# A ninth count table in a graph network's edge aggregation: 117 gather steps in place of 121

## The chip, the core and the metric

The kernel runs on one core of one Trainium2 chip. The metric is the device time of one execution in microseconds, as the median of several runs; before the change it is 1335.8 us. The core's engines are TensorE (PE, with its weight loads as PEld), VectorE (DVE), ScalarE (ACT), GpSimd (POOL) and SyncE (SP). Each works through a queue of its own in order, and they meet at semaphores.

## The reference, cut to what matters

One layer of a graph network with linear attention and a mixture of experts, on 6250 nodes of 256 features and 100,000 edges that are sorted by their target node. The change lies in the graph part:

```
src_f, dst_f = concat(src, loop), concat(dst, loop)
h   = layernorm(x) @ W
deg = segment_sum(1, dst_f);  dinv = rsqrt(deg)
out = segment_sum(h[src_f] * dinv[src_f] * dinv[dst_f], dst_f) + conv_bias
...
x = x + graph(out) + attention(layernorm(x))
x = x + experts(layernorm(x))
```

The target nodes are drawn as 6250 times the square of a uniform number. So the first edges, in sorted order, share few targets, and further on a run of edges spreads over more and more of them.

## The kernel before, in words

Phases follow each other with a barrier between them: loads, degrees and the normed rows z (written to `table` in memory); then the edge phase, lines 719 to 1277, in which the attention and a residual sum are computed beside the edges; then the feature product, the router and the experts. `acc` holds the sums per target node, features on partitions.

The 196 edge groups of 512 edges (four chunks of 128) are summed in two ways.

- **Gathers.** A group is a *step* q of the edge phase: GpSimd gathers the 512 source rows with four indirect DMAs (line 811) into 16 slots, four steps deep, so it waits (`pe_done`) only when it is four steps ahead. VectorE builds four one-hot masks of the targets (`onehots`, line 1045). TensorE multiplies rows and masks, 16 matmul records a step in two halves (`aggregate`, line 828), into a window of 96 nodes. VectorE adds the window to `acc` (`add`, line 1058).
- **Count tables.** For the first groups, where the targets lie close, the edges are counted instead. A table covers one entry of `DBLK` and at most 128 target nodes: `adj`, 128 targets by 6250 sources. For each chunk VectorE builds two one-hots (lines 1073, 1074), TensorE multiplies them (`count`, line 839), and VectorE adds the counts at the chunk's offset (`chunk_add`, line 1088). `DWB` is how many targets a chunk may span. A finished table is multiplied by all of z: 49 products (`product`, line 851), each with 128 rows of z that the sync queue loads in 128 KB pieces into six buffers (`z_rows`, line 775). The result is copied by ScalarE (line 1002), turned by TensorE (line 858) and added to `acc` by VectorE (line 1066). Two buffers `adj` take turns; ScalarE wipes one behind its products (line 958).

Before, eight tables cover groups 0 to 74, and `GQ` = 121 groups go through gathers.

The order is written by hand over the steps. Each engine walks through q = 0 to GQ - 1 and in each through four quarters, and `share(q, lo, hi, n)` deals n items evenly over the steps lo to hi:

- chunks of table b over `BUILT[b]` to `BUILT[b+1]`, its products over `USED[b]` to `USED[b+1]`;
- keys of 49 tiles over steps 0 to 11 (`A0, A1`; line 865 on TensorE, 1099 on VectorE), then setup products at steps 12 and 13;
- keys and values with their context over steps 14 to 33 (`C0, C1`; lines 874 and 881), then a chain of small setup steps at 34 to 36;
- queries of 49 tiles over `B0` to `B1` (lines 888, 896, 902 on TensorE, 1120 to 1145 on VectorE);
- the residual sum over `D0` to `D1`, with one load of x per tile behind the z loads on the sync queue (line 781).

Within a quarter TensorE does counts, attention, products and then, in every second quarter, half of the aggregation. Ahead of the last step the sync queue issues four late loads, after the last table but one has been turned.

Of the kernel before, what the change touches and what calls it, by code (L numbers as in the profile page):

```python
# [7 lines left out]
P = 128  # L8
# [6 lines left out]
T = -(-N // P)  # L15
# [11 lines left out]
OHR = 4  # L27
ECOL = E // P
assert OHB % OHR == 0 and ECOL < NC and E - ECOL * P <= P
DBLK = ((0, 27), (27, 38), (38, 46), (46, 53), (53, 59), (59, 65), (65, 70), (70, 75))  # L30
ND = DBLK[-1][1]
NDB = len(DBLK)
DWB = (5, 5, 6, 7, 8, 8, 8, 9)
DW = max(DWB)
DLIM = P - DW
MD = ND * GC
RUNS = [(min(g0 for (g0, _), k in zip(DBLK, DWB) if k == d), max(g1 for (_, g1), k in zip(DBLK, DWB) if k == d), d)
        for d in sorted(set(DWB))]
assert all((d - 1) * -(-WIN // d) < WIN for d in DWB) and list(DWB) == sorted(DWB) and T * DW <= 512
GQ = NG - ND  # L40
# [27 lines left out]
def build(nc, a_x, a_src, a_dst, a_gw, a_cb, a_lnw, a_lnb, a_pre, a_wqkv, a_mk, a_mv, a_wout, a_bout,  # L68
# [6 lines left out]
    with ExitStack() as ctx:  # L75
        def sb(name, shape, dt=f32):
            return ctx.enter_context(nc.sbuf_tensor(name, shape, dt))
# [11 lines left out]
        R1 = sb("R1", [P, T * D])  # L89
# [4 lines left out]
        zT = R2[:, :].rearrange("p (k n) -> p k n", k=KC)  # L94
        y_all = x_all
        o_all = x_all
        adj = [R1[:, b * T * P:(b + 1) * T * P].rearrange("p (j n) -> p j n", n=P) for b in range(2)]

        def o_tile(t):

# [66 lines left out]
        small = sb("small", [P, 64])  # L167
# [41 lines left out]
        root3, val3, tmp3 = (RG[:, 3660 + 3 * T * k:3660 + 3 * T * (k + 1)] for k in range(3))  # L209
        negmean, total_x = sd[:, :], sa[:, :]  # L210
        iwin_i = slotb[:, 1, 0:P].bitcast(i32)
        cols = sb("cols", [P, 16])
        least, cut, bad = (sb(name, [P, GC]) for name in ("least", "cut", "bad"))
        inblk = S_t[:, :, :, :].rearrange("p s c w -> p (s c w)")[:, 500:500 + P]
        isd = sb("isd", [P, 2])
# [28 lines left out]
        with nc.Block(no_gpsimd_drain=True) as block:  # L244
# [164 lines left out]
            def _(pool):  # L409
                n = 0  # L410

                def step(ins):
                    nonlocal n
                    n += 1
                    ins.then_inc(pl, 1)
                    pool.wait_ge(pl, n)
# [11 lines left out]
                step(nc.gpsimd.memset(inblk, 0.0))  # L428
                for a, b in DBLK:
                    step(nc.gpsimd.tensor_copy(inblk[:, a:b], ident[:, a:a + 1].to_broadcast([P, b - a])))  # L430
# [251 lines left out]

        A0, A1 = 0, 12
        C0, C1 = 14, 34
        B0, B1 = 37, 88
        D0, D1 = 91, GQ - 2
        BUILT = (0, 33, 47, 61, 74, 86, 95, 104, 112)
        USED = (33, 47, 61, 74, 86, 95, 104, 112, GQ - 2)

        def share(q, lo, hi, n):  # L690

            if not lo <= q < hi:
                return range(0)
            return range(n * (q - lo) // (hi - lo), n * (q - lo + 1) // (hi - lo))
# [6 lines left out]
        def chunks(q):  # L701

            for (g0, g1), lo, hi in zip(DBLK, BUILT, BUILT[1:]):
                for m in share(q, lo, hi, (g1 - g0) * GC):
                    yield g0 * GC + m

        def products(q):

            for b in range(NDB):
                for j in share(q, USED[b], USED[b + 1], T):  # L710
                    yield b, j
# [4 lines left out]
        def block_of(m):  # L716
            return next(b for b, (g0, g1) in enumerate(DBLK) if m < g1 * GC)

        phase = later
        with nc.Block(no_gpsimd_drain=True) as block:  # L720
# [96 lines left out]
            def _(pe):  # L817
# [15 lines left out]
                def count(m):  # L833

                    pe.wait_ge(key_ok, m + 1)
                    if m >= 2:
                        pe.wait_ge(cnt_ok, m - 1)
                    wide = T * DWB[block_of(m)]
                    nc.tensor.matmul(psK[m % 2][:, 0:wide], hots[m % 4], hotk[m % 4][:, 0:wide], start=True,  # L839
# [14 lines left out]
                def turn_block(b):  # L854

                    pe.wait_ge(blk_cp, b + 1)
                    for k in range(KC):
                        last = nc.tensor.transpose(psD[:, D + k * P:D + (k + 1) * P], block_rows(b)[:, k, :], ident[:, :])
                    last.then_inc(blk_t, 1)
# [83 lines left out]
                for q in range(GQ):  # L943
                    if q in USED[1:]:
                        turn_block(USED.index(q) - 1)
                    for r in range(4):
# [9 lines left out]
            def _(act):  # L956
# [47 lines left out]
                for q in range(GQ):  # L1004
                    if q in USED[1:] and USED.index(q) - 1 < NDB - 2:
                        b = USED.index(q) - 1
                        act.wait_ge(blk_t, b + 1)
# [30 lines left out]
            def _(v):  # L1038
# [21 lines left out]
                def add_block(b, groups):  # L1060

                    at = nc.vector.value_load(first_i[0:1, DBLK[b][0]:DBLK[b][0] + 1], min_val=0, max_val=N - 1)
                    v.wait_ge(blk_t, b + 1)
                    v.wait_ge(acc_ok, groups)
                    win = acc[:, :, bass.ds(at, P)]
                    nc.vector.tensor_tensor(win, win, halved(psD[:, D:2 * D]), ALU.add).then_inc(blk_ok, 1)

                def chunk_onehots(m):

                    if m >= 4:  # L1070
                        v.wait_ge(cnt_ps, m - 3)
                    wide = T * DWB[block_of(m)]
                    nc.vector.tensor_scalar(hotk[m % 4][:, 0:wide], iokey[:, 0:wide], key[:, m:m + 1], None, ALU.is_equal)
# [187 lines left out]
                for q in range(GQ):  # L1261
                    if q in USED[1:]:
                        add_block(blocks, q - 1)
# [889 lines left out]
```

## Time and profile before

| | |
|---|---|
| median of 3 runs | 1335.8 us (1331.95 to 1337.17) |
| profiled execution | 1330.7 us, span 1329.0 us |
| PE / PEld busy | 1205.2 / 1075.8 us |
| DVE / ACT / POOL busy | 911.8 / 544.3 / 785.8 us |
| gathers in the edge phase (POOL, line 811) | 476, from 126.1 to 738.7 us |
| edge phase | from about 126 to 763 us |
| experts (bound by PE) | from about 926 us to the end |

The chain that ended last is TensorE in the experts, back to 926 us. It does not reach back into the edge phase, which the barrier at 763 us ends, so the edge phase is read from its own rows: by the times of single steps, and by who waits there for whom. The granted clock of TensorE is full from 139 us to the last tables, apart from short stretches.

### The profile page before, as it was taken

To read this page: it belongs to the slowest core of one execution; us is meant where nothing else is said; L and a number is where in the kernel's file an instruction comes from. 1 tells how busy PE (TensorE), PEld (TensorE's weight loads), DVE (VectorE), ACT (ScalarE), POOL (GpSimd) and SP (SyncE) were. 2 spreads that over 40 slices of the span, in tenths; PEclk is the share of its full clock that TensorE was granted. 3 is DMA by queue.
4 is the path that set the end of the run, shared out by engine and by line. 5 is a ranking of instruction groups with operands and counts; after the bars stand their busy time and mean duration, and the time that the engine had idled before them with its cause. 6 is when DMAs were issued, how large, how long until landed. Compare 5 with 4: busy or idle time off the path is not lost. (4 is left out here: it accounts for less than half of the span.)

```text
span 1329.0 us, 29794 instructions
## 1 busy us (share of the span) xinstructions
PE 1205.2 (91%) x8333; PEld 1075.8 (81%) x8334; DVE 911.8 (69%) x2764; ACT 544.3 (41%) x1402; POOL 785.8 (59%) x757
## 2 busy tenths in 40 slices
PE   6974989998999999999898698956999999999998
PEld 6964978887889889887786546944999999999997
DVE  8997987887888777788783268888444444444444
ACT  8737102221333333333311102545555555555553
POOL 7105777777777777777776200002476666666665
PEclk9997999999999999999998899965999999999999
DMA  8026333336666667789898601577254444444443
GB/s 254 0 85 192 100 104 104 104 109 198 195 199 203 200 201 206 209 255 280 268 292 261 218 0 34 173 241 238 53 79 68 70 69 69 70 69 71 71 68 43
DMA packets 138889, 190.11 MB, mean 143 GB/s; under 512 B 22261, under 2 KB 116956, under 8 KB 138532
## 3 DMA queue, kind: packets, MB, share of 16 engines
q0 software_dynamic: 43440, 90.29, 29.4%
q1 hardware_dynamic: 95348, 98.64, 23.4%
q8 instruction: 43, 0.70, 0.2%
q14 instruction: 58, 0.48, 0.1%
HBM read 156.37 MB, written 33.44 MB: 143 GB/s over the span
## 5 line engine op out<-in xcount | busy, mean ns | idle before, releaser
L811 POOL DMA_INDIRECT RG<-table,srci x476 | 465.2, 977 | 149.7 <-issue 139.6
L828 PEld LDWEIGHTS ps<-S_t,RG 128*128 128x128 f32 x1936 | 254.6, 195 | 20.6 <-DMA RG<-table,srci 10.4
L828 PE MATMUL ps<-S_t,RG 128*128 128x96 f32 x1936 | 257.6, 276 | 8.0 <-DMA RG<-table,srci 7.4
L851 PE MATMUL ps<-zrow,R 128*128 128x256 f32 (+1 forms) x784 | 219.9, 388 | 20.1 <-DMA zrow<-table 13.3
L2100 POOL DMA_INDIRECT out<-R,S_t x105 | 166.1, 1582 | 99.3 <-DVE R L2070 55.8
L1983 PE MATMUL ps<-R,RG 128*128 128x128 f32 x1680 | 206.7, 277 | 0.0
L1993 PE MATMUL ps<-R 128*128 x840 | 198.5, 379 | 0.0
L1983 PEld LDWEIGHTS ps<-R,RG 128*128 128x128 f32 x1680 | 197.7, 193 | 0.3 <-issue 0.3
L2016 ACT ACTIVATE R<-ps,RG 128x128 f32<-128x128 f32 x420 | 119.7, 367 | 175.5 <-PE ps L1983 175.5
L1088 DVE TENSOR_TENSOR R<-R,ps 128x245 f32 (+4 forms) x300 | 142.0, 473 | 70.6 <-PE ps L839 45.4
L2066 DVE TENSOR_TENSOR R<-ps,R 128x256 f32<-128x256 f32 x105 | 44.6, 425 | 202.0 <-PE ps L1993 202.0
L851 PEld LDWEIGHTS ps<-zrow,R 128*128 128x128 f32 (+1 forms) x784 | 137.1, 192 | 45.5 <-DMA zrow<-table 23.2
L1993 PEld LDWEIGHTS ps<-R 128*128 128x128 f32 x840 | 151.7, 190 | 16.3
L958 ACT ACTIVATE R<-iwin 128x256 f32<-128x256 f32 (+2 forms) x152 | 71.5, 476 | 186.3 <-PE ps L851 174.7
L2088 POOL DMA_INDIRECT R<-ntable,S_t x105 | 103.9, 990 | 40.2 <-issue 29.3
L2025 ACT ACTIVATE RG<-R 128x1028 f32 x105 | 112.7, 1075 | 9.7 <-PEq L86 9.7
L1678 POOL COPY R<-R 128x8 f32<-128x8 f32 (+1 forms) x13 | 6.0, 474 | 145.8 <-DVEq L1846 126.5
L2055 DVE TENSOR_SCALAR R<-ps,gamma,beta 128x128 f32<-128x128 f32 x212 | 76.2, 400 | 0.0
L487 PE MATMUL ps<-R 128*128 128x49 bf16 x784 | 73.8, 269 | 0.0
L487 PEld LDWEIGHTS ps<-R 128*128 128x128 bf16 x784 | 70.9, 145 | 2.7 <-DVE R L562 2.6
L1045 DVE TENSOR_TENSOR S_t<-dstrel,iwin 128x384 f32<-128x384 f32 x121 | 66.9, 553 | 0.8
L1074 DVE TENSOR_SCALAR ohs<-iokey,slo 128x128 bf16<-128x128 f16 x225 | 61.9, 275 | 0.0
(371 smaller groups left out, 1817.3 us busy)
## 6 DMA issues: line engine op xcount, KB each, us to landing
zrow<-table SPq DMA_DIRECT2D x384, 128.0 KB
RG<-table,srci POOLq DMA_INDIRECT x484, 3.4
ntable<-R SPq DMA_DIRECT2D x12, 516.0 KB, 7.0
out<-R SPq DMA_DIRECT2D x12, 512.0 KB, 3.2
table<-R SPq DMA_DIRECT2D x9, 640.0 KB
R<-in_x SPq DMA_DIRECT2D x6, 896.0 KB, 10.0
R<-in_w SPq DMA_DIRECT2D x8, 514.0 KB, 6.5
slot<-in_x SPq DMA_DIRECT2D x32, 128.0 KB, 4.1
```

What stands on the lines that cost most here:

```text
L487: last = nc.tensor.matmul(ps[7][:, 0:T], ohlo[k][:, :, c], ohhi[k][:, :, c], start=False, stop=False)
L811: nc.gpsimd.indirect_dma_start(out=grows[:, s, :], out_offset=None, in_=table, in_offset=bass.IndirectOffsetOnAxis(ap=srci[:, ND + q, c:c ...
L828: last = nc.tensor.matmul(window(q % 2)[:, h, :], grows[:, s, h * P:(h + 1) * P], S_t[:, q % 2, c, :], start=c == 0, stop=c == GC - 1)
L851: nc.tensor.matmul(psD[:, 0:D], adj[b % 2][0:n, j, :], zrow[0:n, i % ZR, :], start=j == 0, stop=j == T - 1).then_inc(z_used, 1)
L1088: nc.vector.tensor_tensor(win, win, psK[m % 2][:, 0:T * wide].rearrange("p (j w) -> p j w", w=wide), ALU.add).then_inc(cnt_ok, 1)
L1983: last = nc.tensor.matmul(psH[s % 2][:, h * P:(h + 1) * P], w1r[:, s, k * HID + h * P:k * HID + (h + 1) * P], ur[:, s % 2, k, :], start=k ...
L1993: last = nc.tensor.matmul(psY[s % 2][:, 0:D], hr[:, s % 2, h, :], w2_sb[:, bass.ds(e, 1), h, :].rearrange("p a f -> p (a f)"), start=h == ...
L2016: last = act.activation(hr[:, s % 2, h, :], psH[s % 2][:, h * P:(h + 1) * P], ACT.Gelu, bias=w1r[:, s, KC * HID + h:KC * HID + h + 1])
L2025: act.activation(w1r[:, s, :], w1_sb[:, bass.ds(e, 1), :].rearrange("p a f -> p (a f)"), ACT.Copy).then_inc(c_ok, 1)
L2055: nc.vector.tensor_scalar(ur[:, s % 2, k, :], psX[s % 2][:, k * P:(k + 1) * P], gamma[:, k:k + 1], beta[:, k:k + 1], ALU.mult, ALU.add)
L2088: nc.gpsimd.indirect_dma_start(out=xr[:, t % 4, :], out_offset=None, in_=ntable, in_offset=bass.IndirectOffsetOnAxis(ap=gat[:, t:t + 1], a ...
L2100: nc.gpsimd.indirect_dma_start(out=a_out, out_offset=bass.IndirectOffsetOnAxis(ap=sct[:, t:t + 1], axis=0), in_=yr[:, t % 4, :], in_offset ...
```

## The change

The four groups 75 to 78 move from gathers to a ninth table: `ND` goes from 75 to 79, `GQ` from 121 to 117, gathers from 484 to 468, chunks from 300 to 316, products from 392 to 441. With four steps fewer, all that is dealt over steps is dealt anew: the first table is built in 29 steps and not 33, the tables' products run in 12, 12, 11, 10, 10, 9, 8, 7 and 7 steps, where they ran in 14, 14, 13, 12, 9, 9, 8 and 7, and the queries and the residual sum have two steps less each. With an odd number of tables the two `adj` buffers swap places, so that the last table again lies in the upper half of R1, and `cols` moves into `small`. Keys, and keys and values, keep their steps.

```
-DBLK = (..., (65, 70), (70, 75))
+DBLK = (..., (65, 70), (70, 75), (75, 79))
-DWB = (5, 5, 6, 7, 8, 8, 8, 9)
+DWB = (5, 5, 6, 7, 8, 8, 8, 9, 9)
...
-        adj = [R1[:, b * T * P:(b + 1) * T * P].rearrange("p (j n) -> p j n", n=P) for b in range(2)]
+        adj = [R1[:, (b + NDB) % 2 * T * P:((b + NDB) % 2 + 1) * T * P].rearrange("p (j n) -> p j n", n=P) for b in range(2)]
...
-        cols = sb("cols", [P, 16])
+        cols = small[:, 8:17]
...
-        B0, B1 = 37, 88
-        D0, D1 = 91, GQ - 2
-        BUILT = (0, 33, 47, ..., 104, 112)
+        B0, B1 = 37, 86
+        D0, D1 = 89, GQ - 2
+        BUILT = (0, 29, 41, ..., 101, 108)
...
```

What this does to TensorE's order shows at two places. The first is step 31, its first half, in the stretch of the keys and values (L874, context L881), with counts (L839) and the half aggregation (L828) at its end. Before:

```order
L839 MATMUL ps<-ohk,ohs 128x245
L874 MATMUL ps<-wqkv,R 128x256 x2
L881 MATMUL ps<-vsl,esl 128x129
L839 MATMUL ps<-slot,ohs 128x245
L874 MATMUL ps<-wqkv,R 128x256 x2
L881 MATMUL ps<-vsl,esl 128x129
L828 MATMUL ps<-S_t,RG 128x96 x4
```

The same half step on TensorE in the changed kernel:

```order
L839 MATMUL ps<-slot 128x245
L874 MATMUL ps<-wqkv,R 128x256 x2
L881 MATMUL ps<-vsl,esl 128x129
L851 MATMUL ps<-zrow,R 128x256
L839 MATMUL ps<-ohk,ohs 128x245
L874 MATMUL ps<-wqkv,R 128x256 x2
L881 MATMUL ps<-vsl,esl 128x129
L851 MATMUL ps<-zrow,R 128x256
L828 MATMUL ps<-S_t,RG 128x96 x4
```

Two products (L851) of the first table stand between what was there; before, they began at step 33.

The second place is step 70 on TensorE, in the stretch of the queries (L888, with L896 and L902), from its first count to its second half of the aggregation. Before:

```order
L839 MATMUL ps<-slot 128x343
L851 MATMUL ps<-zrow,R 128x256
L888 MATMUL ps<-wqkv,R 128x128 x2
L896 MATMUL ps<-ident,ksl 128x128
L902 MATMUL ps<-wout,vsl 128x256
L851 MATMUL ps<-zrow,R 128x256
L828 MATMUL ps<-S_t,RG 128x96 x4
L839 MATMUL ps<-ohk,ohs 128x343
L851 MATMUL ps<-zrow,R 128x256 x2
L828 MATMUL ps<-S_t,RG 128x96 x4
```

The same step on TensorE in the changed kernel:

```order
L839 MATMUL ps<-slot,ohs 128x392
L851 MATMUL ps<-zrow,R 128x256
L888 MATMUL ps<-wqkv,R 128x128 x2
L896 MATMUL ps<-ident,ksl 128x128
L902 MATMUL ps<-wout,vsl 128x256
L851 MATMUL ps<-zrow,R 128x256 x2
L828 MATMUL ps<-S_t,RG 128x96 x4
L839 MATMUL ps<-slot 128x392
L851 MATMUL ps<-zrow,R 128x256 x2
L828 MATMUL ps<-S_t,RG 128x96 x4
```

The step has five products where it had four, and its chunks belong to a later and wider table (392 columns for 343).

## Rows read from the trace of the kernel before

**Rows 1.** The gathers, line 811: durations in ns, first and last start; idle time's releasers.

```profile
L811 POOL DMA_INDIRECT RG<-table,srci x476: 940/946/1543, 126.1 to 738.7; - x159
...
  issue: 139.6, 458
  PE ps L828: 8.7, 17
```

**Rows 2.** Busy time of each engine in stretches of the edge phase, then clock and DMA.

```profile
core 0: us, PE busy (x) PEld busy (x) DVE busy (x) ACT busy (x) POOL busy (x), PEclk, DMA share, GB/s
139.00:203.00 64.00, 58.53 (x456) 52.21 (x454) 57.92 (x215) 1.43 (x5) 48.77 (x51) 0.97 0.35 103
...
139.00:565.00 426.00, 401.30 (x2810) 362.57 (x2808) 347.56 (x1273) 116.03 (x393) 324.10 (x335) 1.00 0.56 165
372.00:437.00 65.00, 63.78 (x454) 59.31 (x453) 54.47 (x209) 23.99 (x82) 49.46 (x52) 1.00 0.68 203
```

**Rows 3.** Timeline of DVE, adds (steps 0, 12, 28, 33, 36, 40, 47, 59, 85): start, duration.

```profile
139.10 0.35 DVE L1058 TENSOR_TENSOR R<-R,ps 128x192 f32 x1
...
194.97 0.35 DVE L1058 TENSOR_TENSOR R<-R,ps 128x192 f32 x1
...
276.83 0.36 DVE L1058 TENSOR_TENSOR R<-R,ps 128x192 f32 x1 [0.16 <-issue]
...
303.21 0.35 DVE L1058 TENSOR_TENSOR R<-R,ps 128x192 f32 x1
...
318.83 0.36 DVE L1058 TENSOR_TENSOR R<-R,ps 128x192 f32 x1 [0.53 <-issue]
...
340.13 0.35 DVE L1058 TENSOR_TENSOR R<-R,ps 128x192 f32 x1 [0.34 <-issue]
...
376.03 0.36 DVE L1058 TENSOR_TENSOR R<-R,ps 128x192 f32 x1 [0.36 <-issue]
...
431.80 0.35 DVE L1058 TENSOR_TENSOR R<-R,ps 128x192 f32 x1 [0.36 <-issue]
...
565.16 0.36 DVE L1058 TENSOR_TENSOR R<-R,ps 128x192 f32 x1 [0.37 <-issue]
```

**Rows 4.** Timeline of PE, step 50: count, product, queries, product, half an aggregation.

```profile
386.79 0.29 PE L839 MATMUL ps<-ohk,ohs 128*128 128x294 bf16 x1
386.92 0.59 PE L851 MATMUL ps<-zrow,R 128*128 128x256 f32 x2
387.35 0.61 PE L888 MATMUL ps<-wqkv,R 128*128 128x128 f32 x4
...
388.34 0.59 PE L851 MATMUL ps<-zrow,R 128*128 128x256 f32 x2
388.77 1.03 PE L828 MATMUL ps<-S_t,RG 128*128 128x96 f32 x8
389.63 0.29 PE L839 MATMUL ps<-slot,ohs 128*128 128x294 bf16 x1
```

**Rows 5.** Timeline of PE, step 25: from keys and values to what follows their context.

```profile
257.28 1.03 PE L874 MATMUL ps<-wqkv,R 128*128 128x256 f32 x4
...
258.38 1.03 PE L828 MATMUL ps<-S_t,RG 128*128 128x96 f32 x8
```

**Rows 6.** Timeline of DVE, step 12: two chunk adds, the one-hots between them left out.

```profile
187.12 0.41 DVE L1088 TENSOR_TENSOR R<-R,ps 128x245 f32 x1
...
188.01 0.41 DVE L1088 TENSOR_TENSOR R<-R,ps 128x245 f32 x1
```

**Rows 7.** Timeline: adds of steps 94, 103 and 111; turn of the last table.

```profile
611.48 0.34 DVE L1058 TENSOR_TENSOR R<-R,ps 128x192 f32 x1
...
659.55 0.35 DVE L1058 TENSOR_TENSOR R<-R,ps 128x192 f32 x1
...
703.65 0.35 DVE L1058 TENSOR_TENSOR R<-R,ps 128x192 f32 x1
...
752.10 0.69 PE L858 MATMUL ps<-ident,R 128*128 128x128 f32 x2 [2.90 <-ACT R L1002]
```

**Rows 8.** The page's line of the products: busy, mean ns of one, idle before, releasers.

```profile
L851 PE MATMUL ps<-zrow,R 128*128 128x256 f32 (+1 forms) x784 | 219.9, 388 | 20.1 <-DMA zrow<-table 13.3 <-DVE R L1066 5.5 <-DVEq L1200 1.1
```

More of the change, by code:

```diff
@@ L29 @@
 assert OHB % OHR == 0 and ECOL < NC and E - ECOL * P <= P
-DBLK = ((0, 27), (27, 38), (38, 46), (46, 53), (53, 59), (59, 65), (65, 70), (70, 75))
+DBLK = ((0, 27), (27, 38), (38, 46), (46, 53), (53, 59), (59, 65), (65, 70), (70, 75), (75, 79))
 ND = DBLK[-1][1]
 NDB = len(DBLK)
-DWB = (5, 5, 6, 7, 8, 8, 8, 9)
+DWB = (5, 5, 6, 7, 8, 8, 8, 9, 9)
 DW = max(DWB)
@@ L684, in build @@
         C0, C1 = 14, 34
-        B0, B1 = 37, 88
-        D0, D1 = 91, GQ - 2
-        BUILT = (0, 33, 47, 61, 74, 86, 95, 104, 112)
-        USED = (33, 47, 61, 74, 86, 95, 104, 112, GQ - 2)
+        B0, B1 = 37, 86
+        D0, D1 = 89, GQ - 2
+        BUILT = (0, 29, 41, 53, 64, 74, 84, 93, 101, 108)
+        USED = (29, 41, 53, 64, 74, 84, 93, 101, 108, GQ - 2)
         def share(q, lo, hi, n):
```

## The prediction

> **What bounds the kernel now.** I read the page's slices first, then the stretch from 126 to 763 us in which GpSimd gathers, then who waits for whom there. That stretch is the only one that the change alters, and the one after it starts when it is over, so what it gains or loses is gained or lost in the time.
>
> GpSimd issues 476 of its 484 gathers here, and they run without a pause: 458 of its gaps are its own, 139.6 us over all (0.3 us each), and it waited 8.7 us for TensorE [rows 1]. From 126.1 to 738.7 us are 119 steps, 5.15 us each. So GpSimd looks like the bound, and four steps fewer look like 20.6 us. The second look is at TensorE: between 139 and 565 us it is busy for 401.3 of 426 us and VectorE for 347.6 [rows 2]. A matmul's busy time says little of the room left, so I timed the steps by the row with which VectorE adds a step's window to the sums [rows 3]: the adds of steps 0, 12, 28, 33, 36, 40, 47, 59 and 85. Steps 48 to 59 took 55.8 us, 4.65 each, below GpSimd's 5.15: there TensorE caught up on rows that had been gathered long before. Before them it had lost ground: steps 37 to 40 took 5.3 each, 29 to 33 5.3. It has hardly more room than GpSimd.
>
> **Prices.** On TensorE, start to start in a stretch without idle time [rows 4]: a chunk count 0.13 us, a product 0.43, the queries of one tile with the two matmuls behind them 0.99 (387.35 to 388.34), half of a step's aggregation 0.86, so 1.72 a step. Keys and values of one tile with their context take 1.10 (257.28 to 258.38) [rows 5]. On VectorE one chunk (an add and two one-hots) takes 0.89 (187.12 to 188.01) [rows 6]. Check: steps 48 to 59 hold 1.72 + 1.02 x 0.99 + 3.5 x 0.43 + 2.29 x 0.13 = 4.54 us by these prices and took 4.65, so 0.11 a step is not in them.
>
> **The change part by part, against the profiled run.** Removed: four steps, 16 gathers and 4 x 1.72 = 6.9 us of aggregation. Added: 49 products, 21.1 us, 16 counts, 2.1 us, and on VectorE 16 chunks, 14.2 us, less four steps' adds and one-hots. TensorE thus does some 16 us more in four steps less. Where it falls decides.
>
> Steps 1 to 12. The first table's 108 chunks lie in 29 steps instead of 33, 3.72 a step for 3.27. VectorE sets the pace there (busy for 57.9 of 64 us from 139 to 203 [rows 2]), so 12 x 0.45 x 0.89 = +4.8.
>
> Steps 13 to 28, keys and values. Here TensorE waits for ScalarE and VectorE in turn. The same 0.45 chunk costs at least TensorE's 0.13 and at most VectorE's 0.89: 0.06 to 0.40 a step. I take 0.2, since both engines have some room: +3.2 (0.9 to 6.4).
>
> Steps 29 to 33. The first table's products now start at step 29 in place of 33, and the keys and values still run to step 33. A step holds 1.72 + 2.45 x 1.10 + 4.08 x 0.43 + 3.67 x 0.13 = 6.65 us. Five are 33.3; they took 26.4 [rows 3]: +6.9. The gathered rows that wait in four steps' slots would cover this once, if TensorE came there with a lead. It comes 8 us late.
>
> Steps 34 to 36 (a chain of small setup steps between TensorE and VectorE): 0.58 product and 0.53 chunk more each, +1.0. Steps 37 to 40, bound by VectorE with 3.67 chunks for 3.14: 0.53 x 0.89 = 0.47, four times, +2.0. So the add of step 40 comes 17.9 us later, at 358.0.
>
> Steps 41 to 83. The queries run in 49 steps in place of 51, 1.05 us a step. Steps 41 to 52, 53 to 63 and 64 to 83 hold 4.08, 4.45 and 4.9 products each (the second, the third, and the fourth and fifth table), with 2.67, 2.55 and 2.4 chunks: 4.88 us (12 steps), 5.02 (11) and 5.19 (20), each with the 0.11 of the check: 59.9 + 56.4 + 106.0 = 222.3. At a change of table TensorE waited 0.8 us for VectorE (5.5 us in 7 times [rows 8]), four times 3.2. Sum 225.5: the add of step 83 at 583.5. The same point of the work before, with four tables' products left, is the add of step 85 at 565.2: **+18.3 us**, although two steps fewer lie ahead of it. GpSimd alone would have it 10.3 us earlier, so gathers now wait for TensorE.
>
> Steps 84 to the end. Before, these four tables took 46.3, 48.0, 44.1 and 48.5 us [rows 7] in 9, 9, 8 and 7 steps; now 9, 8, 7 and 7. The first was paced by GpSimd. Now rows lie ready, and TensorE needs 9 x (1.72 + 2.34 + 0.29 + 0.23 + 0.11) + 0.8 = 43.0. The others were paced by the rows of z, which come through six buffers and for which TensorE waited 13.3 us on the page [rows 8]. With 8 steps I take the 44.1 of before; with 7 steps and chunks still to build 46 (36 if the rows were there in time, 48.5 as the last table before); the last 48.5. Sum 181.6 for 186.9: **-5.3**. One z load more per row of the table goes to the sync queue ahead of the x tiles; that is in these times.
>
> At no cost: the wipes of one more table (ScalarE waits for products most of the time), the buffers that swap places, the columns moved into another tile, one more mask in the setup, and the four late loads, which keep their place behind the last table but one. If a wipe were late, VectorE's first add of a table would wait, and TensorE with it.
>
> **Sum: +18.3 - 5.3 = +13.0.** The profiled run took 1330.7 us (span 1329.0), 0.4% under the median of 1335.8. I add the difference to the median: **1349 us**. Its own range is 1339 to 1362: steps 13 to 28 at their bounds (-2.3, +3.2), steps 41 to 83 without any wait (-7.9) or with as much as steps 13 to 28 have (5.12 us for 4.84 by the prices, +7), the 7-step table (-10, +2.5). The ends of single terms don't come together, so I cut it there.
>
> **Rivals.** A. GpSimd stays the bound, and the kernel is faster. The waits of TensorE ahead of step 84 are filled by the new products, and the point of step 84 comes 10.3 us earlier by GpSimd's pace, with 5.3 behind it: 1320; all four steps in full give 1315. It holds if the waits that TensorE now has in steps 1 to 36 all but vanish. For it: TensorE's weight loads are busy for 362.6 of 426 us, 85%, against 59.3 of 65 us, 91%, where it ran without a pause [rows 2]: room for 28 us, of which 10 go with the two steps, and the work added by step 83 is 49 x 0.43 + 24 x 0.13 - 2 x 1.72 = 20.8. Against it: that room lies where TensorE waits for a chain, in steps 1 to 36, and new products start at step 29. Chance 0.18.
>
> The Trainium skill, Perfetto Trace Analysis, section Identifying the Most-Contended Engine, says to judge TensorE's headroom by the share of LDWEIGHTS time, not of matmul time. By that rule alone the added work nearly fits and A would come out, at 1320 in place of 1349. The trace agrees that matmul time says little (94% and 98% busy in those two stretches [rows 2]); whether the room can be filled, no row shows.
>
> B. The excess ahead of step 40 is only the 4.8 of VectorE: in steps 13 to 40 products run in the gaps that the chains leave, and 13 us of the sum go. 1336, no difference to be measured. For it: TensorE and VectorE alternate in waiting there, so work for one can lie in the other's time. Against it: 6.65 us of pure work in a step that has 5.15. Chance 0.22.
>
> C. The z rows bind all three last tables: two of 7 steps at 48.5 and the one of 8 at 48, and the first at its old 46.3: +10, 1359. Chance 0.10, on the forecast's side.
>
> That the change does not do what it says is excluded by the program: 468 gathers stand in it, and a chunk's 128 edges near edge 40,000 span some 7 nodes by the reference's distribution, under the nine columns.
>
> **Chances.** Forecast 0.50, C 0.10, B 0.22, A 0.18. About 0.5% is what a measurement tells from no change: faster 0.18, same 0.22, slower 0.60. The range of 1320 to 1364 leaves out the better half of A and the far end of C.
>
> **What would show it.** In the new profile: adds of step 12 near 200 us, of step 33 near 318, of step 40 near 358, of step 83 near 583; GpSimd's waits for TensorE far above 8.7 us; TensorE's waits for gathered rows gone before step 84. If the add of step 83 stands at 555 or less, the prices of steps 29 to 83 are wrong and A holds; an add of step 40 near 345 is B's. If the last four tables take 190 us or more, C is right.

## The result, and the profile after

The changed kernel takes 1353.7 us in the median of 4 runs (1353.4 to 1357.1), beside 1336.0 us before in the same series (1332.0 to 1337.2): a ratio of 1.014, 95% interval 1.012 to 1.016. It is 17.7 us slower; 13 were predicted. The profiled execution has a span of 1351.9 us.

The page's lines of the gathers, the aggregation and the products in the changed kernel, with busy time, mean ns, and the idle time before them with what ended it; of before, [rows 1] has the gathers and [rows 8] the products, and the aggregation's line stands below:

```profile
L811 POOL DMA_INDIRECT RG<-table,srci x460 | 446.2, 970 | 189.3 <-issue 124.7
L828 PE MATMUL ps<-S_t,RG 128*128 128x96 f32 x1872 | 246.6, 276 | 0.2 <-DVE S_t L1045 0.2
L851 PE MATMUL ps<-zrow,R 128*128 128x256 f32 x882 | 245.8, 389 | 25.2 <-DMA zrow<-table 16.9
```

```profile
L828 PE MATMUL ps<-S_t,RG 128*128 128x96 f32 x1936 | 257.6, 276 | 8.0 <-DMA RG<-table,srci 7.4
```

What GpSimd waited for from 126 to 790 us (total us, times, longest):

```profile
POOL RG L811 <- PE ps L828: 63.2, 50, 3.9
```

GpSimd waited 63.2 us for TensorE, where it had waited 8.7, and the aggregation (L828), which waited 7.4 us for gathered rows, waits for none. The products waited 16.9 us for rows of z (13.3 before).

The adds of steps 0, 12, 28, 33, 36, 40, 83, 92, 100 and 107 on VectorE, which answer to [rows 3] and [rows 7] (start, duration), and TensorE's turn of the last table:

```profile
142.34 0.35 DVE L1058 TENSOR_TENSOR R<-R,ps 128x192 f32 x1
...
204.48 0.36 DVE L1058 TENSOR_TENSOR R<-R,ps 128x192 f32 x1
...
290.56 0.36 DVE L1058 TENSOR_TENSOR R<-R,ps 128x192 f32 x1 [0.41 <-issue]
...
322.17 0.35 DVE L1058 TENSOR_TENSOR R<-R,ps 128x192 f32 x1
...
342.00 0.35 DVE L1058 TENSOR_TENSOR R<-R,ps 128x192 f32 x1 [0.52 <-issue]
...
365.00 0.36 DVE L1058 TENSOR_TENSOR R<-R,ps 128x192 f32 x1 [0.36 <-issue]
...
589.36 0.36 DVE L1058 TENSOR_TENSOR R<-R,ps 128x192 f32 x1 [0.37 <-issue]
...
636.78 0.34 DVE L1058 TENSOR_TENSOR R<-R,ps 128x192 f32 x1
...
682.75 0.34 DVE L1058 TENSOR_TENSOR R<-R,ps 128x192 f32 x1
...
727.70 0.35 DVE L1058 TENSOR_TENSOR R<-R,ps 128x192 f32 x1
...
775.23 0.69 PE L858 MATMUL ps<-ident,R 128*128 128x128 f32 x2 [2.92 <-ACT R L1002]
```

Differences of these rows and of those of before give the stretches (us):

| steps | before | predicted | after |
|---|---|---|---|
| 1 to 12 | 55.9 | 60.7 | 62.1 |
| 13 to 28 | 81.9 | 85.1 | 86.1 |
| 29 to 33 | 26.4 | 33.3 | 31.6 |
| 34 to 36 | 15.6 | 16.6 | 19.8 |
| 37 to 40 | 21.3 | 23.3 | 23.0 |
| 41 to 83 (before: to 85) | 225.0 | 225.5 | 224.4 |
| from there to the last turn | 186.9 | 181.6 | 185.9 |
| **first add to last turn** | **613.0** | **626.1** | **632.9** |

So 19.9 us were lost from the first add on: 21.0 up to step 83, and 1.1 came back. Another 3.2 us of the difference between the two profiles is a later first add (142.34 for 139.10), which is not the change's (last section).

Busy times (PE, PEld, DVE, ACT, POOL, with counts), granted clock, DMA share and GB/s of the changed kernel in steps 29 to 33, 34 to 36, 41 to 83 and in the last four tables. A granted clock of 1.00 is the higher of its two levels, 2.4 GHz, and 0.50 the lower, 1.2 GHz; 0.91 is a mean of both:

```profile
290.56:322.17 31.61, 31.61 (x212) 28.61 (x211) 21.21 (x75) 10.13 (x33) 18.25 (x20) 1.00 0.56 164
322.17:342.00 19.83, 15.25 (x95) 12.79 (x94) 13.62 (x51) 2.90 (x7) 12.31 (x14) 0.91 0.57 169
365.00:589.36 224.36, 222.17 (x1509) 203.61 (x1509) 190.22 (x682) 84.04 (x286) 165.61 (x172) 1.00 0.73 216
589.36:775.20 185.84, 161.61 (x945) 136.08 (x944) 117.91 (x330) 49.50 (x113) 116.32 (x118) 0.97 0.87 266
```

TensorE is busy for all of steps 29 to 33 and for 99% of steps 41 to 83. In the last tables it idles for 24 us.

### The profile page after: what moved, and what is told of

It reads as the page before. It is cut to its first block and busy times, and to the rows that moved or that the text cites. A ratio compares the mean times of both kernels' runs of the same rounds, so it can differ in the third digit from the quotient of the medians.

```text
span 1351.9 us, 30078 instructions
## 1 busy us (share of the span) xinstructions
PE 1222.7 (90%) x8385; PEld 1086.9 (80%) x8386; DVE 926.2 (69%) x2805; ACT 551.7 (41%) x1428; POOL 775.8 (57%) x742
## 5 line engine op out<-in xcount | busy, mean ns | idle before, releaser
L811 POOL DMA_INDIRECT RG<-table,srci x460 | 446.2, 970 | 189.3 <-issue 124.7
L851 PE MATMUL ps<-zrow,R 128*128 128x256 f32 x882 | 245.8, 389 | 25.2 <-DMA zrow<-table 16.9
L828 PEld LDWEIGHTS ps<-S_t,RG 128*128 128x128 f32 x1872 | 247.1, 196 | 10.0 <-DVE S_t L1045 0.6
L828 PE MATMUL ps<-S_t,RG 128*128 128x96 f32 x1872 | 246.6, 276 | 0.2 <-DVE S_t L1045 0.2
L1088 DVE TENSOR_TENSOR R<-R,ps 128x245 f32 (+4 forms) x316 | 151.4, 479 | 73.3 <-PE ps L839 48.1
L851 PEld LDWEIGHTS ps<-zrow,R 128*128 128x128 f32 x882 | 154.5, 192 | 56.6 <-DMA zrow<-table 29.8
L958 ACT ACTIVATE R<-iwin 128x256 f32<-128x256 f32 (+2 forms) x177 | 81.6, 467 | 207.7 <-PE ps L851 191.7
L839 PE MATMUL ps<-ohk,ohs 128*128 128x245 bf16 (+4 forms) x158 | 47.5, 302 | 26.0 <-DVE ohs L1074 21.5
L1074 DVE TENSOR_SCALAR ohs<-iokey,slo 128x128 bf16<-128x128 f16 x237 | 66.8, 282 | 0.0
```

The source lines that it names most:

```text
L811: nc.gpsimd.indirect_dma_start(out=grows[:, s, :], out_offset=None, in_=table, in_offset=bass.IndirectOffsetOnAxis(ap=srci[:, ND + q, c:c ...
L828: last = nc.tensor.matmul(window(q % 2)[:, h, :], grows[:, s, h * P:(h + 1) * P], S_t[:, q % 2, c, :], start=c == 0, stop=c == GC - 1)
L851: nc.tensor.matmul(psD[:, 0:D], adj[b % 2][0:n, j, :], zrow[0:n, i % ZR, :], start=j == 0, stop=j == T - 1).then_inc(z_used, 1)
L958: return act.activation(adj[b % 2][:, j:j + n, :], iwin[:, :].unsqueeze(1).to_broadcast([P, n, P]), ACT.Copy, scale=0.0)
L1088: nc.vector.tensor_tensor(win, win, psK[m % 2][:, 0:T * wide].rearrange("p (j w) -> p j w", w=wide), ALU.add).then_inc(cnt_ok, 1)
```

## The experiments

The theory: up to step 83 TensorE, with VectorE, sets the pace and GpSimd no longer does; what is lost by step 40 stays lost; the last four tables wait for rows of z. Steps are timed from the add of step 0, so that the different starts fall out.

**1. No gathers behind the fourth step, in the changed kernel.**

```
-                for q in range(EARLY, GQ):
+                for q in range(EARLY, 4):
...
-                            pe.wait_ge(got[s], (q // 4) * 16 + 16)
+                            pe.wait_ge(got[s], 16)
```

> The changed kernel, with gathers issued for the first four steps only; every later step multiplies the rows of those steps again, so the gathered rows of later steps are left out of the computation. TensorE's and VectorE's work is unchanged, GpSimd and its transfers are idle. Theory (TensorE, with VectorE, sets the pace up to step 83): the add of step 83 stays 447 us behind that of step 0, 3 us either way, and the last four tables, which wait for rows of z, gain at most 15 us from the transfers that are gone. Rival (the gathers still set the pace somewhere before step 83, through GpSimd or through the transfers that they share with the rows of z): the add of step 83 comes 10 us or more earlier.

Measured: 1330.7 us. The adds of steps 0 and 83:

```profile
139.65 0.34 DVE L1058 TENSOR_TENSOR R<-R,ps 128x192 f32 x1
...
585.63 0.36 DVE L1058 TENSOR_TENSOR R<-R,ps 128x192 f32 x1 [0.36 <-issue]
```

The add of step 83 stands 446.0 us behind the first (447.0 with the gathers): no gather sets the pace there. From step 83 to the last turn it took 166.0 us in place of 185.9, a gain of 19.8 where at most 15 were expected: without the gathers' traffic the wait for rows of z falls from 16.9 to 5.7 us.

**2. The same edit in the kernel before.**

> The kernel before with the same edit: gathers for the first four steps only, the rows of later steps left out of the computation. Theory: here the gathers did set the pace in places, so the add of step 85, 426 us behind that of step 0, comes 8 to 18 us earlier: the waits for rows go, TensorE's work stays. The first of the last four tables, 46.3 us, falls to about 43. Rival (the gathers were no bound before either, and the change lost only by added TensorE work): the add of step 85 moves less than 3 us.

Measured: 1306.6 us. The adds of steps 0 and 85:

```profile
142.68 0.35 DVE L1058 TENSOR_TENSOR R<-R,ps 128x192 f32 x1
...
559.62 0.36 DVE L1058 TENSOR_TENSOR R<-R,ps 128x192 f32 x1 [0.37 <-issue]
```

The add of step 85 stands 416.9 us behind the first, 9.1 earlier than with gathers (426.1). All but 1.1 of it arises behind step 60: before, the rows gathered ahead were used up there, and GpSimd set the pace. The first of the last four tables took 44.9 us (46.3), not the 43 expected.

Put side by side, the two runs split the loss up to step 83. Without gathers the changed kernel needs 445.98 - 416.94 = 29.04 us more: that is what the added work costs on TensorE and VectorE, with the waits of one for the other. The gathers add 1.05 us to it, where they added 9.12 to the kernel before. 29.04 + 1.05 - 9.12 = 20.97. The change did free GpSimd, but that was worth 8 us, and it paid 29.

**3. Rows of z loaded once, in the changed kernel.**

```
                     if i >= ZR:
                         sp.wait_ge(z_used, i - ZR + 1)
+                    if i >= ZR:
+                        return
...
-                    pe.wait_ge(z_in[i % ZR], i // ZR * 16 + 16)
+                    pe.wait_ge(z_in[i % ZR], 16)
```

> The changed kernel, with the rows of z loaded into the six buffers once and never again; later products multiply whatever lies there, so 435 of 441 loads of z and the right products are left out of the computation. Theory: up to step 83 nothing waits for z rows and the time is the same, 447 us from the first add to that of step 83, 5 us either way; the last four tables, which measured 186 us, fall to 155 to 165, since then TensorE's work, some 4.7 us a step at 5 to 7 products, is all that is left. Rival (traffic of the z loads slows gathers and so TensorE throughout): the add of step 83 comes 10 us or more earlier. Rival (the last tables are bound by TensorE's work as well): they stay above 178 us.

Measured: 1331.2 us. Step 83 at 446.5 us (447.0): the transfers of z slow nothing before it. From there to the last turn 155.5 us in place of 185.9. So 30 us of the last tables come with the loads of z. Here the last gathers became late instead, as what TensorE waited for most from 589 to 760 us shows (total us, times, longest):

```profile
PE ps L830 <- DMA RG<-table,srci: 7.1, 4, 3.0
```

**4. The first table's products cut to 8 columns, in the changed kernel.**

```
+                    w = 8 if b == 0 and 0 < j < T - 1 else D
-                    nc.tensor.matmul(psD[:, 0:D], adj[b % 2][0:n, j, :], zrow[0:n, i % ZR, :], ...
+                    nc.tensor.matmul(psD[:, 0:w], adj[b % 2][0:n, j, :], zrow[0:n, i % ZR, 0:w], ...
```

> The changed kernel, with 47 of the 49 products of the first table cut from 256 columns to 8; their waits, weight loads and rows of z stay, the rest of those products is left out of the computation. These are the products that now begin at step 29, among the keys and values. Two records of a product start 0.43 us apart at 256 columns; at 8 columns the weight load is what is left, by the records of 96 columns at most 0.22. So TensorE's work in steps 29 to 40 falls by 10 us or a little more. Theory (TensorE's columns are what made steps 29 to 40 late): the add of step 41 comes 8 to 12 us earlier, and most of that is still there at step 83. Rival (VectorE's chunks or the weight loads set the pace there): at most 3 us at step 41. Rival (it is made up later, the queries being bound by something else): 8 to 12 us at step 41, under 3 us at step 83.

Measured: 1357.4 us. Step 33 came 3.7 us earlier, step 41 only 1.2. None of the three cases can be read from it, because the clock moved. Busy times in steps 29 to 33, 34 to 36 and 37 to 40; the granted clock is the number before the last two:

```profile
291.31:319.10 27.79, 27.24 (x215) 25.70 (x215) 20.76 (x74) 9.86 (x33) 18.69 (x20) 1.00 0.63 188
319.10:339.15 20.05, 16.37 (x84) 15.43 (x84) 13.71 (x51) 2.90 (x7) 11.81 (x14) 0.60 0.56 164
339.15:364.42 25.27, 21.81 (x141) 20.93 (x140) 18.88 (x74) 5.71 (x17) 17.22 (x18) 0.78 0.60 180
```

With the clock at 0.60 and 0.78 the lighter steps 34 to 40 took longer than the full ones (45.3 us for 42.8). The experiment is void; the next one asks the question the other way round.

**5. The first table's products done twice, in the changed kernel.**

```
+                    if b == 0 and 0 < j < T - 1:
+                        nc.tensor.matmul(psD[:, 0:D], adj[0][0:n, j, :], zrow[0:n, i % ZR, :], start=False, stop=False)
```

> The changed kernel, with 47 of the 49 products of the first table done twice, so that this table is added to the sums twice over: that is the part that changes in the computation. TensorE has 47 x 0.43 = 20.2 us more to do in steps 29 to 40 and is never less busy than before, so that its clock has no reason to fall; nothing else is added. Theory (TensorE sets the pace of steps 29 to 33 and, with the set-up chain and VectorE, of steps 34 to 40): steps 29 to 33 grow by 5 x 4.08 x 0.43 = 8.8 us, one for one, steps 34 to 40, where TensorE now idles for some 8 us, by 4 to 11, and all of it, 13 to 20 us, is still there at step 83. Rival (VectorE sets the pace from step 29 to 40): under 6 us at step 40. Rival (there is room behind step 40 in which it is caught up): under 6 us at step 83.

Measured: 1363.2 us. Busy times in steps 29 to 33, 34 to 36, 37 to 40 and 41 to 83:

```profile
290.64:330.53 39.89, 39.89 (x248) 35.81 (x246) 21.41 (x74) 9.95 (x33) 18.37 (x20) 1.00 0.44 128
330.53:350.34 19.81, 18.66 (x121) 16.25 (x120) 13.74 (x52) 2.97 (x8) 12.18 (x14) 1.00 0.63 169
350.34:376.32 25.98, 25.40 (x168) 22.80 (x167) 19.20 (x73) 5.47 (x18) 16.07 (x17) 1.00 0.61 173
376.32:600.74 224.42, 222.23 (x1509) 203.67 (x1509) 190.21 (x683) 84.10 (x286) 165.93 (x173) 1.00 0.72 216
```

Steps 29 to 33 grew by 8.3 us, with 20 more products in that stretch, 8.6 us at 0.43 each: TensorE sets their pace, nearly one for one. Steps 34 to 36 did not move (19.8) with 12 more products, 5.2 us, in them: TensorE's waits there fell from 4.4 to 1.1 us, and its clock was 1.00 in place of 0.91. Steps 37 to 40 grew by 3.0. The sum at step 40 is 11.3 us, under the 13 to 20 expected, since I had not seen how much of steps 34 to 36 is waiting; at step 83 it is 11.4. What is lost by step 40 is carried, to a tenth, past 43 more steps. Behind step 83 4 us of it came back, where the last tables wait for transfers anyway.

**6. VectorE's chunk adds of the first two tables cut to 5 columns, in the changed kernel.**

```
-                    win = adj[b % 2][:, :, bass.ds(at, wide)]
+                    tiles = 1 if b < 2 else T
+                    win = adj[b % 2][:, 0:tiles, bass.ds(at, wide)]
```

> The changed kernel, with VectorE's chunk adds of the first two tables cut from 245 columns to 5; the counts for the other 240 columns are left out of the computation, the one-hots and TensorE's counts stay. One add took 0.41 us, and what is left may take 0.1 to 0.15, so VectorE has 1.0 us less to do in each of the steps 1 to 40. Theory (VectorE's chunks set the pace of steps 1 to 12, share in steps 13 to 28, and hold TensorE up in steps 34 to 40; in steps 29 to 33 TensorE is busy without a gap): the add of step 12, 62.1 us behind that of step 0, comes 5 to 9 us earlier, steps 13 to 28 (86.1) gain 2 to 6, steps 29 to 33 (31.6) under 1, steps 34 to 40 (42.9) 2 to 6, and from there the lead stays, 8 to 20 us at step 83. Rival (TensorE sets the pace in steps 13 to 40 as well, or the chain of keys, values and setup does): the gain is under 10 us at step 40 and comes from steps 1 to 12 alone.

Measured: 1348.5 us. Steps 1 to 12 gained 2.5 us (59.7), steps 13 to 28 2.8, steps 29 to 33 0.1, steps 34 to 40 1.5; 6.9 at step 40, 5.2 at step 83. VectorE has a part in the early steps, but a smaller one than I expected: its busy time in steps 1 to 12 fell from 55.3 to 44.9 us and the time by 2.5. Behind VectorE stands TensorE, which in these steps waits for several small things in turn (counts, keys, setup). The rival (under 10 us at step 40) has the size right, not the place.

**7. The early chunk pace alone, in the kernel before.**

```
-        BUILT = (0, 33, 47, 61, 74, 86, 95, 104, 112)
+        BUILT = (0, 29, 47, 61, 74, 86, 95, 104, 112)
```

> The kernel before, with the first table's chunks dealt over steps 0 to 28 in place of 0 to 32, and everything else as it was: its products still begin at step 33, but the second table's chunks begin at step 29 and are thinner. This is the part of the change that quickens VectorE's work early, alone. Theory (VectorE's pace in steps 1 to 28 costs some 9 us, and is worth that only where it is not caught up): the add of step 28, 137.7 us behind the first, comes 8 to 11 us later, and by step 47, with fewer chunks from step 29 to 46 and rows gathered ahead, 0 to 4 us later. Rival (ground lost in steps 1 to 28 is lost for good): still 8 us or more later at step 47 and at step 85. Rival (the early chunks cost nothing and the lateness of the changed kernel at step 28 is from its later start): under 3 us at step 28.

Measured: 1341.5 us (one run; before 1334.8 in that series). Step 28 stands 147.3 us behind the first, 9.6 later than before (137.7), so the chunk pace is nearly all that the changed kernel lost there (10.5). By step 46 the lag is 1.7 us, as the theory said, since the second table's chunks are thinner here. But at step 85 it is 4.7, a case that I had not foreseen: GpSimd, four steps ahead with all slots full, had waited for TensorE more often. Its waits up to 375 us, here and in the kernel before:

```profile
POOL RG L811 <- PE ps L828: 11.3, 11, 1.5
```

```profile
POOL RG L811 <- PE ps L828: 2.3, 5, 1.1
```

So the rows run short earlier: in steps 48 to 59 TensorE waited 2.3 us for them (0.2 before), and from step 55 on the lag grows again.

**8. The first table dealt over 34 steps, in the changed kernel.**

```
-        BUILT = (0, 29, 41, 53, 64, 74, 84, 93, 101, 108)
-        USED = (29, 41, 53, 64, 74, 84, 93, 101, 108, GQ - 2)
+        BUILT = (0, 34, 45, 56, 66, 76, 85, 93, 101, 108)
+        USED = (34, 45, 56, 66, 76, 85, 93, 101, 108, GQ - 2)
```

> The changed kernel, all work kept, dealt otherwise: the first table is built in 34 steps in place of 29, so that its products begin behind the keys and values, and the tables behind it run their products in 11, 11, 10, 10, 9, 8, 8, 7 and 6 steps. Nothing overlaps at steps 29 to 33, and VectorE's chunks are fewer a step. Theory (TensorE's total of work up to the last tables sets the time; the overlap only decides where it is late): the run is 3 to 8 us faster than the changed kernel, 0.2 to 0.6%, and still slower than the kernel before by 0.8% or more: steps 34 to 85 then pay with 0.3 to 0.4 products a step more. Rival (the overlap at steps 29 to 33, with the faster chunks ahead of it, is the whole of the loss): 15 to 20 us faster, at the time of the kernel before.

Measured: 1356.1 us (1350.5 to 1356.9), ratio to before 1.015 (1.012 to 1.018): no faster than the changed kernel. Its adds of steps 0, 33, 40, 83 and 92:

```profile
143.77 0.35 DVE L1058 TENSOR_TENSOR R<-R,ps 128x192 f32 x1
...
308.26 0.35 DVE L1058 TENSOR_TENSOR R<-R,ps 128x192 f32 x1
...
351.12 0.35 DVE L1058 TENSOR_TENSOR R<-R,ps 128x192 f32 x1 [0.34 <-issue]
...
586.58 0.36 DVE L1058 TENSOR_TENSOR R<-R,ps 128x192 f32 x1 [0.36 <-issue]
...
636.99 0.34 DVE L1058 TENSOR_TENSOR R<-R,ps 128x192 f32 x1
```

Against the changed kernel it is 15.3 us ahead at steps 33 and 40, 4.2 at step 83, and 1.2 at step 92, when both have finished the same tables. The overlap at steps 29 to 33 is thus not the loss; it only shows it early. The rival of 15 to 20 us falls, and my 3 to 8 was too much.

**9 and 10. A seventh buffer for rows of z, in the kernel before and in the changed one.** The buffer lies over two constant tiles that GpSimd builds again for the router.

```
-ZR = 6
+ZR, ZB = 7, 6
...
-        ones = sb("ones", [P, P])
-        tri = sb("tri", [P, P])
+        pair_m = sb("onestri", [P, 2 * P])
+        ones, tri = pair_m[:, 0:P], pair_m[:, P:2 * P]
...
+        def z_buf(k, n):
+            return zrow[0:n, k, :] if k < ZB else pair_m[0:n, :]
...
+                    if i == ZB:
+                        sp.wait_ge(mid_pe, 2)
```

> The kernel before, with a seventh buffer for rows of z, laid over two constants that the edge phase does not use and that are rebuilt by GpSimd before they are used again. All work is kept. Theory (the last tables wait because only six pieces of z are on the way at a time, so a seventh brings a sixth more in the same latency): the last three tables, 48.0, 44.1 and 48.5 us, shrink by 9 to 15 us together, and the run is 0.6 to 1.1% faster than the kernel before. Rival (the transfers themselves are at their limit there): no gain above 2 us, within 0.3%.

> The changed kernel with the same seventh buffer for rows of z. Theory (the last four tables, 185.8 us, are held by the six buffers, and TensorE alone needs about 160): 10 to 18 us off them, which brings the changed kernel to the time of the kernel before, within 0.7%, but not under that of the kernel before with a seventh buffer. Rival (the transfers are at their limit): no gain above 2 us.

Measured: the kernel before with seven buffers 1329.3 us, ratio 0.996 (0.994 to 0.998); the changed kernel with seven 1339.6 us, 1.004 (1.002 to 1.006), both against the kernel before. TensorE's waits for rows of z in the last tables of the changed kernel, with seven buffers:

```profile
PE ps L856 <- DMA zrow<-table: 3.1, 6, 1.1
PE ps L856 <- DMA onestri<-table: 2.4, 4, 1.1
```

The wait falls from 16.9 to 5.5 us, and the time from step 83 to the last turn from 185.9 to 169.5: the number of pieces on the way held these tables, and the transfers were not at their limit. The gain lies in the last three; the first of the four still took 46.6 us (47.4). In the kernel before, the same buffer brings 7.2 us there (186.9 to 179.7). The last three shrank by 10.8 us, as expected (9 to 15). But the first took 49.9 us in place of 46.3, and the gathered rows are what is late there, 3.4 of the 5.8 us that TensorE waits for them in the four:

```profile
PE ps L833 <- DMA RG<-table,srci: 5.8, 6, 2.4
...
PE ps L856 <- DMA zrow<-table: 3.6, 6, 0.8
```

With most of the wait for z gone the two kernels still differ by 10.3 us. The kernel before with seven buffers beats both kernels; its 0.4% is under the 0.6 to 1.1% expected.

## Why the prediction was right, and where its sizes were off

**Right.** Slower, 1354 for 1349, by the mechanism forecast. By the signs it named: step 12 at 204.5 (near 200), step 33 at 322.2 (318), step 40 at 365.0 (358), step 83 at 589.4 (583.5); each is 3.2 us nearer if the later start is taken off. GpSimd waits 63.2 us for TensorE, and the aggregation's waits for rows are gone.

**The prices of TensorE held.** Steps 41 to 83 were put together from single rows: 225.5 us, measured 224.4, and not by luck of the sum: steps 41 to 52, 53 to 63 and 64 to 83 took 60.2, 56.4 and 107.8 us for 60.7, 57.2 and 107.6. That stretch, a third of the edge phase, decided that four steps fewer bring nothing there.

**The terms up to step 40** sum to 21.6 us where 17.9 were predicted, with errors of both signs. The chunks' price was too low in steps 1 to 12 (+6.3 for +4.8) and 13 to 28 (+4.2 for +3.2). Products at steps 29 to 33 were too high (+5.2 for +6.9): TensorE had no gap left, as forecast, yet needed 6.32 us a step and not 6.65.

**Mis-sized: steps 34 to 36**, +1.0 predicted, +4.2 measured. I had added TensorE's work for products and chunks, and put longer waits and the clock at nothing. TensorE's waits there and the count that follows the next half aggregation (that one took 1.86 us for the 1.03 of [rows 4]), in the changed kernel and then before:

```profile
326.62 0.27 PE L839 MATMUL ps<-slot 128*128 128x245 bf16 x1 [2.04 <-DVE R L1088]
...
335.33 0.90 PE L851 MATMUL ps<-zrow,R 128*128 128x256 f32 x2 [2.39 <-DVEq L1200]
...
337.09 1.86 PE L828 MATMUL ps<-S_t,RG 128*128 128x96 f32 x8
338.75 0.41 PE L839 MATMUL ps<-ohk,ohs 128*128 128x245 bf16 x1
```

```profile
306.38 0.27 PE L839 MATMUL ps<-slot 128*128 128x245 bf16 x1 [0.88 <-DVE R L1088]
...
310.63 0.27 PE L839 MATMUL ps<-slot,ohs 128*128 128x245 bf16 x1 [0.62 <-DVE R L1088]
...
313.75 0.70 PE L851 MATMUL ps<-zrow,R 128*128 128x256 f32 x2 [1.08 <-DVEq L1200]
...
315.69 0.27 PE L839 MATMUL ps<-ohk,ohs 128*128 128x245 bf16 x1
```

The waits are 4.4 us for 2.6, so 1.8 more. The longest ends with VectorE's set-up copy (line 1199), and in VectorE's order a chunk now stands ahead of that copy, which before followed the add of step 35 at once. VectorE in the changed kernel, then before:

```profile
334.12 0.41 DVE L1088 TENSOR_TENSOR R<-R,ps 128x245 f32 x1 [0.82 <-issue]
...
334.81 0.42 DVE L1199 COPY wout<-ps 128x256 f32<-128x256 f32 x1
```

```profile
312.81 0.35 DVE L1058 TENSOR_TENSOR R<-R,ps 128x192 f32 x1
313.21 0.42 DVE L1199 COPY wout<-ps 128x256 f32<-128x256 f32 x1
```

Experiment 7, which deals only chunks anew, has a chunk at that place too, and the same wait of 2.4 us for the copy. Right behind the wait the granted clock fell to 0.50 and stayed there from 335.7 to 339.1 us: from the product behind the copy to the count behind the half aggregation, the same matmuls took 3.42 us for 1.94, 1.5 more. The changed kernel and its variants of experiments 1, 3, 6 and 10 show 0.91 as the clock of these steps, the kernel before and its variants 1.00. What is left, 0.9 us, is about the +1.0 of the forecast. Why the clock fell stays open: in experiment 8 TensorE waited 4.9 us in these steps, at a clock of 1.00.

**Mis-sized: the last four tables**, -5.3 predicted, -1.1 measured. The failed step is the first of them, of which it was said that the rows lie ready and TensorE needs 43.0. The gathered rows did lie ready, but the table took 47.4 us. Without the loads of z it took 43.5, and without gathers 44.5: TensorE's work was rightly priced, and what I left out is that in this table, too, the rows of z come late beside the gathers. TensorE's wait for them from 589.4 to 636.8 us (0.3 in the kernel before):

```profile
PE ps L851 <- DMA zrow<-table: 1.9, 2, 1.4
```

Its weight loads waited 3.8 us there (0.9 in experiment 1). A seventh buffer took only 0.8 us off this table, so the number of buffers is not what held it; why the rows come late there stays open. The others came to 46.0, 45.0 and 47.5 for 44.1, 46 and 48.5.

**Rival A** (GpSimd stays the bound) fell with experiment 1. The Trainium skill's rule in Perfetto Trace Analysis, section Identifying the Most-Contended Engine, on LDWEIGHTS time as TensorE's headroom, would have given it. The trace does not bear it out: where TensorE ran without a gap, weight loads were busy for 28.61 of 31.61 us and, with products doubled, for 35.81 of 39.89, 91 and 90%, as in the full stretch of [rows 2]. So the 91% that the prediction took for a full TensorE was right, but the average of 85% hides that the room lies in steps that wait for chains, while the new products stand where there was none. **Rival B** fell with steps 29 to 33, in which TensorE was busy for all of the 31.6 us. **Rival C** was right on the first table alone (47.4 for 46.3).

**What stays open.** From the first add on, the profiles differ by 19.9 us and the medians by 17.7; with the later start they differ by 22.9. The profiled execution of before was 5.3 us under its median; an early start, as in that profile, would explain 3.2 of that, and the other 2.1 are less than the spread of the runs (5.2). When the runs without a profile started is not on record.

## What to carry to other kernels

Where work moves from one engine to another, count what the relieved engine made others wait for, not what it did: 16 gathers and four steps were 20.6 us of GpSimd's time, but up to the last four tables all the gathers together cost only 9 us of time, and TensorE, 94% busy, paid for the work in their place. An engine that loses time early in a stretch where it is then 99% busy carries the loss to the end of it, and the new deal of the same work in experiment 8 brought nothing. And a wait for transfers is worth one more buffer before it is worth a new algorithm: by the medians the seventh buffer took 5 us off the kernel before and 14 off the changed one.

## What the runs showed of the hardware that was not expected

**The first early gather takes 1.3 or 4.7 us.** Just ahead of the edge phase GpSimd issues eight gathers (line 466), while VectorE makes 17 copies (line 654). In the changed kernel, and then in the kernel before:

```profile
112.53 5.79 DVE L654 COPY R<-R 128x512 f32<-128x512 f32 x17
114.78 4.64 POOL L466 DMA_INDIRECT RG<-table,srci  x1 [8.80 <-DMA table<-R]
```

```profile
112.38 5.87 DVE L654 COPY R<-R 128x512 f32<-128x512 f32 x17
114.28 1.33 POOL L466 DMA_INDIRECT RG<-table,srci  x1 [8.47 <-DMA table<-R]
```

In ten of twelve profiles the first gather took 4.6 to 4.9 us and ended about 1.1 us behind the last copy; in two (the kernel before and experiment 1) it took 1.3 to 1.4 and the edge phase began 3 us earlier. Both kernels show both, so it is no part of the change. It fits what the Trainium skill says in SBUF — State Buffer, section SBUF: two separate sides, that a VectorE copy of 32-bit data within SBUF shuts GpSimd out of a port that they share, so that its descriptors are written late. In the two fast profiles, though, the gather ran beside the same copies in 1.3 to 1.4 us, so that alone does not tell the cases apart. No run here moved the copies, so the cause was not tested.

**Less work, a lower clock.** With products of 8 columns (experiment 4, one run) TensorE still counted as busy for 27.2 of 27.8 us in steps 29 to 33; its granted clock then fell to 0.60 over the next 20 us, most of the time at the lower of its two levels, and to 0.78 over the 25 behind them, where the full kernel had 0.91 and 1.00. The seven steps with some 28 thin products in them took 2.5 us longer than with the full ones. To ask what a matmul costs, doubling it was the better experiment than thinning it.
